# A three-layer graph attention kernel: VectorE's one-hots read their numbers from PSUM, and four small products of TensorE's softmax chain change

## The reference

```python
def _gatv2_layer(x, src, dst, n, Wl, Wr, att, b):      # layers 1 and 2: 4 heads of 64, with self-loops
    xl = (x @ Wl).reshape(n, H, C)
    xr = (x @ Wr).reshape(n, H, C)
    e = jax.nn.leaky_relu(xl[src] + xr[dst], NEG_SLOPE)
    logits = jnp.einsum('ehc,hc->eh', e, att)
    m = jax.ops.segment_max(logits, dst, num_segments=n)
    ex = jnp.exp(logits - m[dst])
    denom = jax.ops.segment_sum(ex, dst, num_segments=n)
    alpha = ex / (denom[dst] + 1e-16)
    msg = xl[src] * alpha[:, :, None]
    out = jax.ops.segment_sum(msg, dst, num_segments=n)
    return out.reshape(n, H * C) + b
```

## Time and profile before

| | |
|---|---|
| median of 3 runs | 4124.04 us (4122.51 to 4126.01) |
| the profiled execution | 4115.89 us, span 4114.1 us |
| mean granted clock of TensorE | 0.947 |
| TensorE matmuls | busy 3659.4 us, 89% |
| VectorE | busy 3149.5 us, 77% |
| GpSimd | busy 2804.3 us, 68% |
| ScalarE | busy 1229.2 us, 30% |
| DMA | 521 MB, 127 GB/s |

### The profile page before, as it was taken

One profiled execution on the slowest core, in us unless ns is written; L12 is line 12 of the kernel. 1 busy time (PEld: TensorE's weight loads), 2 busy tenths in 40 slices (PEclk: granted clock), 3 DMA queues, 4 the chain that ended last, 5 costly groups with the idle time before them and its releaser, 6 DMA issues. The chain is left out here.

```text
span 4114.1 us, 121899 instructions
## 1 busy us (share of the span) xinstructions
PE 3659.4 (89%) x31817; PEld 2722.7 (66%) x31818; DVE 3149.5 (77%) x8748; ACT 1229.2 (30%) x4200; POOL 2804.3 (68%) x2941
## 2 busy tenths in 40 slices
PE   6699999999999898999999999977788777877875
PEld 5577777777776676777777777745455554555543
DVE  6667877787788665787787787875688788888886
ACT  4433333333333563333333333324111111111113
POOL 5577777777775127777777777723777777777760
PEclk9899999999999999999999999999788889888889
DMA  4354444444443225444444444435545545554544
GB/s 101 107 141 127 132 131 133 127 132 132 132 127 96 62 67 135 131 132 132 127 132 132 131 126 132 126 107 176 136 136 139 137 132 139 139 135 133 139 107 125
DMA packets 333899, 521.05 MB, mean 127 GB/s; under 512 B 152887, under 2 KB 219617, under 8 KB 333809
## 3 DMA queue, kind: packets, MB, share of 16 engines
q0 software_dynamic: 120320, 338.39, 30.1%
q1 hardware_dynamic: 213489, 181.58, 15.4%
HBM read 484.14 MB, written 35.46 MB: 126 GB/s over the span
## 5 line engine op out<-in xcount | busy, mean ns | idle before, releaser
L692 POOL DMA_INDIRECT gathered<-table,idx x2496 | 2610.5, 1046 | 800.1 <-issue 545.9
L1131 PE MATMUL pS<-gathered,Dm 128*128 128x264 f32 x4992 | 1706.2, 425 | 90.6 <-DVE Dm L1537 49.4
L1525 DVE TENSOR_TENSOR acc_mem<-acc_mem,pS 128x264 f32 x2496 | 1041.4, 417 | 133.0 <-PE pS L1131 108.7
L1068 PE MATMUL pZ<-DT,x 128*128 128x128 bf16 x9984 | 1083.7, 221 | 11.8 <-DVE DT L1488 9.0
L1068 PEld LDWEIGHTS pZ<-DT,x 128*128 x9984 | 867.9, 99 | 339.4 <-issue 61.6
L853 ACT ACTIVATE reluT<-pZ 128x256 f32<-128x256 f32 x1664 | 636.9, 383 | 1301.8 <-PE pZ L1074 1182.5
L1074 PE MATMUL pZ<-ident,gathered 128*128 128x128 f32 x3328 | 937.5, 282 | 15.9 <-DMA gathered<-table,idx 15.7
L1131 PEld LDWEIGHTS pS<-gathered,Dm 128*128 128x128 f32 x4992 | 793.0, 200 | 234.1 <-DVE gathered L1554 112.6
L1554 DVE TENSOR_TENSOR gathered<-gathered 128x512 f32<-128x512 f32 x1248 | 852.4, 683 | 65.0 <-ACT gathered L870 64.1
L1537 DVE TENSOR_TENSOR Dm<-iota_row,rel_items 128x256 f32<-128x256 f32 x1248 | 516.5, 414 | 0.0
L1074 PEld LDWEIGHTS pZ<-ident,gathered 128*128 128x128 f32 x3328 | 470.7, 141 | 20.3 <-DMA gathered<-table,idx 18.9
(11 more groups left out here) (230 smaller groups left out, 3372.3 us busy)
## 6 DMA issues: line engine op xcount, KB each, us to landing
DT<-rel_dram SPq DMA_DIRECT2D x156, 512.0 KB
gathered<-table,idx POOLq DMA_INDIRECT x2496
flags<-flag_dram SPq DMA_DIRECT2D x1664, 8.0 KB
span_row<-flag_dram SPq DMA_DIRECT2D x1664, 0.1 KB
table<-xls SPq DMA_DIRECT2D x147, 132.0 KB, 1.9
flags<-flag_dram SPq DMA_DIRECT2D x416, 32.0 KB
gathered<-table SPq DMA_DIRECT2D x98, 132.0 KB, 2.1
gathered<-in_x SPq DMA_DIRECT2D x98, 128.0 KB, 2.1
```

Of the source, the lines that this page charges most:

```text
L692: nc.gpsimd.indirect_dma_start(out=G[:, b, i, :], out_offset=None, in_=tab[l], in_offset=bass.IndirectOffsetOnAxis(ap=idx[:, b, i:i + 1], ...
L1068: mm = nc.tensor.matmul(z_slot(i)[:, half], x3[:, bass.ds(tk[i], 1), s, half].rearrange("p o c -> p (o c)"), moving, start=(s == 0), stop= ...
L1131: nc.tensor.matmul(pS[:, i % 4, 0:ROW], Dm[:, i % 8, :], G[:, at[0], at[1], :], start=True, stop=True).then_inc(seg_done, 1)
L1525: link(v.tensor_tensor(acc_at(n), acc_at(n), pS[:, n % 4, 0:ROW], ALU.add))
```

## The change

The numbers 0 to 127 are copied once, in front of layer 0's edge phase, into columns 288 to 415 of all four banks of `pS`. In every step that also adds a product, L1537 reads them from the bank that the add just in front of it has emptied, instead of from `iota_row`. Four products of the chain change: `lin` is added by a transposing matmul; of F1 and B1 only column 0 is turned, into one row; `carry_in` has its two rows at partitions 0 and 32 of one tile and is turned by one matmul with two columns of the identity; and the turning of dif and mT moves from behind the expansion and in front of the weighted matmul of item 6 to in front of that item's expansion.

```diff
-        carry_in = sb("carry_in", [P, 2, 8 * GI])
+        carry_in = sb("carry_in", [P, 8 * GI])
...
                         freed = (l < 2 or i % 4 == 0) and (late if i <= GI // 2 else second)
+                        if second and i == 6:
+                            pe.wait_ge(dif_ready, up(dif_ready))
+                            nc.tensor.transpose(pM[:, P:2 * P], dif[:], ident[:])
+                            nc.tensor.transpose(pM[:, 0:P], mT[:], ident[:]).then_inc(dif_turned, 1)
                         if first and l < 2:
                             expand(i, freed)
...
-                            nc.tensor.matmul(pL[:, 0:P], lin[:], ident[:],
+                            nc.tensor.matmul(pL[:, 0:P], lin[:], ident[:], is_transpose=True,
                                              start=False, stop=True).then_inc(logits_done, 1)
...
-                                nc.tensor.transpose(pM[:, 0:P], F1[:], ident[:])
-                                nc.tensor.transpose(pM[:, P:2 * P], B1[:], ident[:]).then_inc(ends_turned, 1)
+                                nc.tensor.transpose(pM[0:1, 0:P], F1[:, 0:1], ident[:])
+                                nc.tensor.transpose(pM[0:1, P:2 * P], B1[:, 0:1], ident[:]).then_inc(ends_turned, 1)
                             if i == 4:
                                 pe.wait_ge(carry_ready, up(carry_ready))
-                                for r in range(2):
-                                    mm = nc.tensor.matmul(pM[:, 256 + r:257 + r], carry_in[:, r, :], ident[:, 0:1], start=True, stop=True)
-                                mm.then_inc(carry_turned, 1)
-                            if i == 6:
-                                pe.wait_ge(dif_ready, up(dif_ready))
-                                nc.tensor.transpose(pM[:, P:2 * P], dif[:], ident[:])
-                                nc.tensor.transpose(pM[:, 0:P], mT[:], ident[:]).then_inc(dif_turned, 1)
+                                nc.tensor.matmul(pM[:, 256:258], carry_in[:], ident[:, 0:33:32], start=True, stop=True).then_inc(carry_turned, 1)
...
                     clear_sums()
+                    dve.wait_ge(xr_ready, TILES)
+                    dve.wait_ge(xls_ready, TILES)
+                    pre(v.tensor_copy(pS[:, :, IOTA:IOTA + P], iota_row[:].unsqueeze(1).to_broadcast([P, 4, P])))
...
-                            ins = v.tensor_tensor(Dm[:, 2 * p % 8:2 * p % 8 + 2, :], iota_row[:].unsqueeze(1).to_broadcast([P, 2, P]),
+                            numbers = pS[:, 2 * s % 4, IOTA:IOTA + P] if adds else iota_row[:]
+                            ins = v.tensor_tensor(Dm[:, 2 * p % 8:2 * p % 8 + 2, :], numbers.unsqueeze(1).to_broadcast([P, 2, P]),
                                                   rel.unsqueeze(2).to_broadcast([P, 2, P]), ALU.is_equal)
...
-                                    ins = v.tensor_copy(heads_first(carry_in[0:1, r, :]), in_turns(row))
+                                    ins = v.tensor_copy(heads_first(carry_in[32 * r:32 * r + 1, :]), in_turns(row))
...
+IOTA = 288
```

More of the change, by code:

```diff
@@ L1578, in body @@
                                 if l == 2:
-                                    ins = v.tensor_copy(carry_in[0:1, r, :].rearrange("o (h k) -> o h k", h=H), row)
+                                    ins = v.tensor_copy(carry_in[32 * r:32 * r + 1, :].rearrange("o (h k) -> o h k", h=H), row)
                                 else:
-                                    ins = v.tensor_copy(heads_first(carry_in[0:1, r, :]), in_turns(row))
+                                    ins = v.tensor_copy(heads_first(carry_in[32 * r:32 * r + 1, :]), in_turns(row))
                             ins.then_inc(carry_ready, 1)
```

## The result

The changed kernel takes **4164.4 us** (median of 4 runs, 4163.6 to 4165.7) against 4124.8 (4122.5 to 4126.0): a ratio of 1.0095, 95% interval 1.0083 to 1.0108. It is 40 us slower, where 60 us less were forecast. Its profiled execution has a span of 4163.8 us.

What follows compares the result with a forecast made beforehand. Gathers bound the third layer, gathers and TensorE together the first two. Savings of 41.6, 15.6 and 3 us less a 0.7 us copy made 60 us: 4064 from 4124.0, own range 4050 to 4085 (47%), wider range 4015 to 4114.

Steps and rivals of the forecast that it cites:

- The bound: Edge phases: gathers bind the third layer; gathers and TensorE bind the first two side by side, 21.6 us a group.
- the first two terms of the sum: Gathers freed from the one-hots: 104 groups x 0.40 = 41.6 us in layers one and two, 52 x 0.30 = 15.6 in three.
- The hold: Gathers starting inside a VectorE instruction with two SBUF inputs wait until it ends; beside one PSUM input they don't.
- The holds of L1554 stay at 3.0 to 3.5: VectorE's scaling, L1554, would still catch 3 to 3.5 gathers a group, costing 1.0 us a group as before.
- The rival: Slower case, 7%: gathers lock to VectorE's rhythm, 5.5 L1554 catches a group at 1.8 us, deciding from 4.2; 4186 us.
- TensorE's terms: TensorE, first two layers: lin -0.16, carry_in -0.23, F1 and B1 +0.13, item 7 wait -0.33; -0.6 us a group.
- The bound of -1.0: Best case of TensorE's sum: 0.21, 0.23, 0.33 and some 0.25 for slow matmuls behind the stall, us a group.
- VectorE's two copies into `carry_in`: VectorE: the second copy, now into partition 32, costs 0 to 0.2 us a group, taken as 0.1, covered by idle time.
- dif and mT: Transposes moved ahead of item 6's expansion: exponent 0.8 us earlier, L1554's 0.63 us wait for it closes.
- the forecast's other half: With the earlier exponent, L1554's 0.63 us wait closes and TensorE's 0.33 us wait for L1554 at item 7 goes.
- Landings: TensorE at 21.0 us a group, gathers at 21.2: the rest of TensorE's gain becomes waiting for gathers to land.
- The ends of the layers: Softmax chain after each layer's last gather shorter by some 1 us, three times: 3 us saved.

Runs made afterwards that it cites:

- e1: Kernel before with only the one-hots' numbers read from PSUM: 4115.5 us (ratio 0.9986).
- e3: Changed kernel with the scaling's weights also read from PSUM, after two small VectorE copies a group: 4074.9 us (ratio 0.9885).
- e4: Kernel before with only the scaling's weights read from PSUM, after two small VectorE copies a group: 4098.8 us (ratio 0.9948).
- e13: Kernel before with both one-hots and scaling reading from PSUM, TensorE's products as before: 4078.2 us (ratio 0.9893).
- e8: Changed kernel with the scaling's weights from PSUM and ScalarE's exponent ahead of item 6's relu: 4004.5 us (ratio 0.9709).
- e15: Kernel before with the single carry_in product and its two copies alone: 4096.0 us (ratio 0.9932).
- e11: Changed kernel with VectorE comparing the one-hots twice at step 6 of every group: 4138.9 us (ratio 1.0048).
- e5: Kernel before with the lin, F1/B1 and carry_in changes only; dif and mT not moved, one-hots from SBUF: 4113.5 us (ratio 0.9978).
- e10: Changed kernel with VectorE comparing the one-hots twice at step 5 of every group: 4113.2 us (ratio 0.9977).

## Why the prediction was wrong, step by step

**The bound (failed in part).** "The gathers never stand still", and that TensorE runs beside them at the same pace, were both right. But the sum took the gathers' gain at full size for 104 groups because TensorE's own gain was to make room for it. e1 has the gathers' gain alone and gets 7 us (4115.5 for 4122.2) of the 57 that the first two terms of the sum name; in its trace layers 0 and 1 get 1 and 3.

**The hold (right).** Two SBUF inputs hold a gather, one PSUM input doesn't. L1539 holds none: of the 115 gathers of the changed kernel that start inside it alone, the longest takes 0.950 us. e3, e4 and e13 show the same of the scaling. The Trainium skill ("SBUF — State Buffer", Who interferes with whom) infers that `tensor_tensor` doesn't disturb the making of descriptors. The traces disagree as far as these gathers go: one input moved to PSUM took 89 us off the changed kernel (e3). Which part of a gather is held, its reading of the indices or its writing of descriptors, no run here shows.

**The holds of L1554 stay at 3.0 to 3.5 (failed; this is the loss).** They went to 5.3, 5.2 and 4.2. I took a hold as a chance event whose number is the same wherever VectorE stands; the rows allowed more. The earlier trace rows have two L1554 1.61 us apart, and the earlier trace rows the 0.305 us gap: 0.82 + 0.305 = 1.125 lies inside the second. The rival's price of 1.8 us a group was right. Its threshold was a little high: layer 2 lost 14 us at 4.2 holds, since each was 0.35 us and no longer 0.30, and those of L1486 grew too. The 7% were too few for what the rows allowed. The rival's source was another, too. It had the scaling take over what the one-hots let go, and with the one-hots' holds gone alone the scaling's don't grow in layers 0 and 1 (e1: 3.1 by 0.24 us), and in layer 2 only from 3.5 to 4.0; the products bring the growth.

**TensorE's terms.** lin: from its first matmul to the next instruction 0.325 us before, 0.165 now, so -0.16 as said. carry_in: 0.468 to 0.244, -0.22 for -0.23. F1 and B1: 0.218 in both, so 0 for the +0.13 taken. (Each is the median of 46 or 47 groups of layer 1.) The bound of -1.0 had 0.25 us for matmuls that are slow behind the stall; L1131 at item 7 takes 0.60 us to the next start in the kernel before and also in e8, where the stall is gone, so no run shows that term. The 21.0 us a group that the sum came to is what e8 runs at.

**VectorE's two copies into `carry_in` (mis-sized).** The prediction took 0.1 us a group and at most 0.2. From the start of one instruction to the next the two took 0.10 us each before, and take 0.29 and 0.25 now (median of 46 groups of layer 1), 0.32 us more. The rows of before, then of after; the first are the neighbours of the earlier trace rows:

```profile
2014.06 0.21 DVE L1581 COPY carry_in<-Bout 1x64 f32<-1x64 f32 x1
2014.16 0.41 DVE L1525 TENSOR_TENSOR acc_mem<-acc_mem,pS 128x264 f32 x1
```

```profile
2017.36 0.27 DVE L1583 COPY carry_in<-Fout 1x64 f32<-1x64 f32 x1
2017.64 0.21 DVE L1583 COPY carry_in<-Bout 1x64 f32<-1x64 f32 x1
2017.89 0.43 DVE L1526 TENSOR_TENSOR acc_mem<-acc_mem,pS 128x264 f32 x1
```

They lie between the scalings of steps 1 and 2, whose ends are 2.82 us apart in layers 0 and 1 instead of 2.50, and at 2.8 us every hold was passed on. How much of the loss that makes wasn't isolated: e15 has these copies too, and is faster than before.

**dif and mT (failed).** "ScalarE's exponent then comes 0.8 us earlier" is the step: it came 0.1 to 0.2 us later in the median, and 0.5 to 0.6 in the mean. I followed TensorE's queue and not ScalarE's, where the relu of item 6 stands a few lines ahead of the exponent. With ScalarE's order changed too, it is 0.7 us earlier than before, and the forecast's other half comes true: the wait of 0.63 closes, the stall at item 7 goes, and 55 to 70 us come back. The third layer has no such relu, and there it is 0.53 us with and without the move.

**Landings.** TensorE's waits for them appear as said (13.5 us in 900), but as part of the slower gathers, not behind faster ones.

**The ends of the layers (not seen).** The sum had 3 us there and 0.7 for the copy of the numbers. The copy took 0.70. What lies outside the three runs of gathers grew by 4.5 us between the two profiled executions, where 3 less were forecast.

**What stays open.** The rule says which hold is passed on, given where the scalings stand. It does not say which gather is the first to be held in a group, and so not why the holds of layer 0 need the move and the products together, nor why two products shift layer 2. e11 shows that one can miss there even with the rule in hand. The traces do show that the holds are a pattern that repeats group after group. In the stretches of layers 0 and 1 the scalings of steps 3, 6 and 0 (of the next group) hold a gather, and no others, in 78 of 84 groups of the kernel before; in 72 of 83 groups of the changed one it is those of steps 2, 4, 5, 7 and 1, in half of them that of step 0 as well. e15 has the first pattern in 81 of 84 groups. e5 has the first in 61 of 85 and the second in 21, which may be why its runs scatter by 33 us; that is a guess, since one execution of it was traced. What puts a kernel into one pattern or the other was not found.

## What to carry to other kernels

When an engine with a fixed gap after each instruction can be held by another's, don't count the holds and keep their number: lay the period of the one over the spacings of the other, and see which spacing passes a hold on. If possible remove what holds (here one input moved to PSUM, 89 us) before shortening anything nearby, since a shortening can move the phase: four smaller products took the holds from 3.0 to 5.3 a group. And when a product is moved ahead on one engine, read the queue of the engine that consumes it: what stands ahead there must move too.

## What the runs showed of the hardware

- A gather (0.945 us, 128 rows of 264 f32) that starts inside a VectorE instruction with two SBUF inputs ends 0.82 us behind it; the next starts 0.305 us later. Holds can so follow VectorE's spacing for several instructions, and 0.45 us of added VectorE work a group took 51 us off the whole (e10). VectorE's L1486 holds gathers too, with one large input in SBUF (a `tensor_scalar`, 128x2048 bf16, 0.79 us): all 150 that start inside it alone in the changed kernel end 0.78 to 0.84 us behind it.
- VectorE took the same time from PSUM as from SBUF: the one-hots' 128x256 comparison 414 ns in both kernels, the 128x512 scaling 0.68 us in e8 and in the changed kernel.
- Two copies of one row each (1x64 f32) on VectorE, into partition 0 of one tile, took 0.10 us each to the next start; with the second into partition 32 they took 0.29 and 0.25 us (0.22 and 0.25 in e15).
- A transpose with one column of weights and one row out took TensorE as long as one of 128 x 128: 0.11 us to the next start (the changed kernel's matmuls below; the earlier trace rows for L1117 to L1118).

```profile
2015.95 0.27 PE L1112 MATMUL pM<-ident,F 128*1 128x128 f32 x1
2016.06 0.27 PE L1113 MATMUL pM<-ident,B 128*1 128x128 f32 x1
```
